# Two neighbouring units in one buffer, loaded by one 2 MB transfer with 4 KB rows

## The reference

```python
Ws = 0.5 * (W + jnp.swapaxes(W, -1, -2))
A = jax.nn.sigmoid(U @ U.T)
K = Ws * A[None, :, :]
deg = jnp.maximum(K.sum(axis=-1), EPS)
d = jax.lax.rsqrt(deg)
K = K * d[:, :, None] * d[:, None, :]
out = layernorm(x + w_scale * jnp.einsum('bnm,bmc->bnc', K, x))
```

## Time and profile before

| | us |
|---|---|
| median of 3 runs | 492.47 |
| lowest, highest | 489.37, 500.56 |
| the profiled execution | 489.78 |
| its span from first to last instruction | 487.9 |

### The profile page before, as it was taken

The page is one execution under the profiler, slowest core; times in us unless marked ns, Lnnn a source line. Parts: engine busy times, 40 slices in busy tenths (PEclk is TensorE's granted clock), DMA queues, the critical chain, the costliest instruction groups (busy, mean ns, idle before and its releaser), DMA issues.

```text
span 487.9 us, 14490 instructions
## 1 busy us (share of the span) xinstructions
PE 447.6 (92%) x5318; PEld 236.5 (48%) x5318; DVE 417.0 (85%) x1154; ACT 209.9 (43%) x655; POOL 113.4 (23%) x133
## 2 busy tenths in 40 slices
PE   7888899999989999999999999799998999899893
PEld 6556344555435553565354554454445544455352
DVE  6897467899699988999899998799889998799745
ACT  3886232554335442554335532454434542444420
POOL 0000011003330225103330234103330225103452
PEclk9996699999999999999999999999999999989998
DMA  8999299986999799996999699976999689984012
GB/s 290 387 330 350 81 362 368 359 301 221 358 343 324 259 321 362 375 326 236 362 380 358 212 380 364 351 241 244 387 345 343 261 322 361 356 253 170 2 41 47
DMA packets 101387, 143.11 MB, mean 293 GB/s; under 512 B 35824, under 2 KB 35824, under 8 KB 101360
## 3 DMA queue, kind: packets, MB, share of 16 engines
q1 hardware_dynamic: 86496, 139.01, 80.7%
q10 hardware_dynamic: 14864, 3.74, 3.6%
HBM read 138.54 MB, written 4.19 MB: 293 GB/s over the span
## 4 chain that ended last, share of the span: by engine, by line
PE 61%; DMA 14%; DVE 12%; issue 8%; ACT 2%; SPq 1%; POOL 0%; DVEq 0%; POOLq 0%
PE yp L437 35%; DMA k<-in_adj_dram 14%; PE tw L395 10%; PE kt L395 9%; DVE k L666 6%; DVE k L677 3%; PE yp L535 3%; PE yp L470 2%; ACT k L559 1%; ACT gate L546 1%; SPq L251 1%; DVE deg_parts L677 1%; DMA h<-in_L_gnn_U_dram 1%; PE kt L481 1%; PE kt L535 0%
## 5 line engine op out<-in xcount | busy, mean ns | idle before, releaser
L559 ACT ACTIVATE k<-kt 128x512 f32<-128x512 f32 (+3 forms) x288 | 149.5, 524 | 234.1 <-PE kt L395 233.8
L437 PE MATMUL yp<-k,z 128*64 128x512 f32 x944 | 239.6, 615 | 4.9 <-DVE z L697 2.6
L666 DVE TENSOR_TENSOR k<-tw,k 128x512 f32<-128x512 f32 (+2 forms) x320 | 193.4, 604 | 41.9 <-PE tw L395 28.5
L677 DVE CUSTOM_DVE_ANT_0 k<-k,gate 128x512 f32<-128x512 f32 (+2 forms) x320 | 198.5, 620 | 0.0
L395 PEld LDWEIGHTS kt<-ident,k 64*128 64x128 f32 x1920 | 75.4, 142 | 86.3 <-issue 86.1
L395 PEld LDWEIGHTS tw<-ident,k 64*128 64x128 f32 x2176 | 83.5, 141 | 67.0 <-issue 65.7
L395 PE MATMUL kt<-ident,k 64*128 64x64 f32 x1920 | 94.2, 232 | 19.5 <-DVE deg_parts L677 13.5
L395 PE MATMUL tw<-ident,k 64*128 64x64 f32 x2176 | 101.7, 230 | 4.5 <-DMA k<-in_adj_dram 1.7
L437 PEld LDWEIGHTS yp<-k,z 128*64 128x64 f32 x944 | 56.4, 137 | 73.1 <-issue 60.0
L327 POOL TENSOR_TENSOR d<-deg,minus_half 128x4 f32<-128x4 f32 x32 | 32.5, 1015 | 222.1 <-DVE deg L687 221.4
L559 ACT ACTIVATION_READ_ACCUMULATOR k<-kt 128x1 f32 x288 | 57.2, 198 | 0.0
(11 more groups left out here) (53 smaller groups left out, 138.7 us busy)
## 6 DMA issues: line engine op xcount, KB each, us to landing
k<-in_adj_dram SPq DMA_DIRECT2D x128, 1024.0 KB, 7.4
xt<-in_x_dram ACTq DMA_DIRECT2D x7, 512.0 KB, 7.6
out_dram<-h SPq DMA_DIRECT2D x7, 512.0 KB, 7.0
xt<-in_x_dram SPq DMA_DIRECT2D x1, 512.0 KB, 14.5
out_dram<-k SPq DMA_DIRECT2D x2, 128.0 KB, 2.1
out_dram<-k SPq DMA_DIRECT2D x3, 64.0 KB, 1.7
h<-in_L_gnn_U_dram SPq DMA_DIRECT2D x1, 128.0 KB, 3.2
out_dram<-k ACTq DMA_DIRECT2D x1, 64.0 KB, 1.9
```

What stands on the lines that cost most here:

```text
L437: t = pe.matmul(yp[at:at + C, m // 2, :], z[:, n * G + c, :], K[(n, m)][:, c, :], start=(q == first_unit[m] and c == 0), stop=(q == last_u ...
L559: nc.scalar.activation(K[(j, i)][:, r, c0:UW].rearrange("p (c h e) -> p c h e", h=2, e=H), whole_rows(kt[:, 0:2, :], r % 2, (UW - c0) // P ...
L666: nc.vector.tensor_tensor(row, whole_rows(tw[:, tw_bank[g] // 2 * 2:tw_bank[g] // 2 * 2 + 2, :], g % 2, w // P), row, ALU.add).then_inc(su ...
L677: nc.vector.tensor_tensor_reduce(row, row, A[:, A_AT[g]:A_AT[g] + w], 1.0, 0.0, ALU.mult, ALU.add, deg_parts[:, i * G + r, j:j + 1]).then_ ...
```

## The change

From batch 1 on, the two units of a pair are loaded by one transfer of 2 MB into one buffer, `wide`, of 128 partitions by 4 rows by 1024, in which both are views; a run in HBM is then 1024 floats (4 KB) in place of 512 (2 KB). One semaphore tells of the pair. A consumer of either unit waits for the whole pair. Batch 0 is still loaded by units, but its last four loads come in another order and with other waits, since the shared memory is laid out anew.

```diff
+FIRST_LOADS = [n for n in FIRST_LOADS if n not in ((2, 2), (2, 3), (3, 2), (3, 3))] + [(3, 2), (3, 3), (2, 3), (2, 2)]
...
-LOADS = [(0, 1), (0, 0)] + [u for pair in PAIRS[1:] for u in pair]
...
-        place = [(2, 2), (3, 3), (3, 2), (2, 3)]
-        place += [n for n in FIRST_LOADS if n not in place]
-        K = {n: sb(f"k_{n[0]}{n[1]}", [P, G, UW]) for n in place}
+        wide_place = [(2, 2), (3, 2)]
+        wide_place += [pair[0] for pair in PAIRS if pair[0] not in wide_place]
+        wide = {n: sb(f"k_{n[0]}{n[1]}", [P, G, 2 * UW]) for n in wide_place}
+        K = {(i, j + k): wide[(i, j)][:, :, k * UW:(k + 1) * UW] for i, j in wide_place for k in range(2)}
...
-        loaded = {n: sem(f"loaded_{n[0]}{n[1]}") for n in LOADS}
+        loaded = {n: sem(f"loaded_{n[0]}{n[1]}") for n in FIRST_LOADS}
+        wide_loaded = {n: sem(f"wide_loaded_{n[0]}{n[1]}") for n in wide_place}
+
+        def wait_loaded(engine, b, n, first):
+            if first:
+                engine.wait_ge(loaded[n], 16)
+            else:
+                engine.wait_ge(wide_loaded[PAIRS[PAIR_OF[n]][0]], b * 16)
...
-                if n in ((3, 2), (2, 3)):
+                if n in ((3, 2), (3, 3)):
                     sp.wait_ge(ut_done, 8)
-                if n in ((2, 2), (3, 3)):
+                if n in ((2, 2), (2, 3)):
                     sp.wait_ge(uu_done, NL)
                 load_unit(0, n)
             def load_pair(b, q):
                 sp.wait_ge(prod_done, b * NQ + (q + 1 - NQ))
-                for n in (LOADS[0:2] if q == 0 else PAIRS[q]):
-                    load_unit(b, n)
+                i, j = PAIRS[q][0]
+                src = adj[b, i * UW:(i + 1) * UW, j * UW:(j + 2) * UW].rearrange("(g p) m -> p g m", p=P)
+                sp.dma_start(wide[(i, j)][:, :, :], src).then_inc(wide_loaded[(i, j)], 16)
...
                 if r == 0:
-                    pe.wait_ge(loaded[(j, i)], b * 16 + 16)
+                    wait_loaded(pe, b, (j, i), first)
...
                 if r == 0:
-                    dve.wait_ge(loaded[STEPS[s]], b * 16 + 16)
+                    wait_loaded(dve, b, STEPS[s], first)
```

More of the change, by code:

```diff
@@ L657, in copy_u, with add_row @@
                 nc.vector.tensor_copy(ut_columns(ut_a, k), ut_bank(2 * k)).then_inc(ut_a_copied, 1)
-            def add_row(b, g):
+            def add_row(b, g, first):
                 s, r = LOWER[g]
@@ L748, in steps @@
                 for g in range(NL):
-                    add_row(b, g)
+                    add_row(b, g, lags == 1)
                     if lags == 1:
```

## The result

The changed kernel takes 544.3 us (median of 4 runs, 541.72 to 548.75), the kernel before 492.6: the ratio is 1.117, with a 95% interval from 1.109 to 1.126. It is slower, in the way that was forecast, but by more: the profiled execution took 542.0 us, where the sum said 531.0, and 1.117 times the time before is 550 us, past the range's 546. Some executions of the changed kernel and of its relatives are longer throughout; the ratios leave them out, and where a median holds some of them the ratio is the better number.

What follows compares the result with a forecast made beforehand. TensorE, VectorE and the DMA engines were taken as nearly full, with nothing to soak up new waits. 489.78 + 31.2 (waits) + 6.8 (clock) + 3.2 (batch 0) = 531.0 us, range 505 to 546.

Steps and rivals of the forecast that it cites:

- The late first unit: Waits for a pair's first unit at rows 4, 12, 16, 28: rows 12, 16, 28 start 2.0, 3.1, 5.3 us later.
- the transfers as the bound: Rival, whole loop: longer rows let the DMA queue run ahead, VectorE's 13.4 us of waits go; 474 us, chance 0.05.
- The idle time: Rival, whole loop: VectorE's 3.3 idle us a period swallow the delays; 493 us, chance 0.06.
- only row 28 counts: Rival, rows 12 to 28: TensorE running ahead makes up rows 12 and 16; 7 x 2.2 us remain, 508 us, chance 0.10.
- Rows of 4 KB do move as packets of 4 KB: Rival, pair loads: claimed the reverse, rows still moved in 2 KB packets, no speed gained; 536 us, chance 0.05.
- half of the 14 as falls: TensorE's two gaps a batch: seven clock falls, five more than now, at 1.35 us each; 6.8 us.
- The rival with all 14: Rival, TensorE's gaps: the clock falls at every gap, 20.4 us; 545 us, chance 0.12.
- The waits were 31.2: Batches 1 to 7: two undisturbed batches 5.1 us longer each, five others 4.2 us each; 31.2 us together.
- 7.55 was said: Pair loads: a pair of 2 MB lands 7.55 us after its issue; ends 5.1 and 7.8.
- lands at 254.9: Row 12, batch 4: q4's load, issued at 246.5, queues behind q3's and lands 5.13 us after it, at 254.9.
- The allowance of 0.9 us: Five batches with a full queue: first units already late, so each grows by 4.2 us where undisturbed ones grow by 5.1.
- Batch 0 was taken at +3.2: Batch 0, TensorE's row 28: unit (2,3) lands at 49.4, 3.2 us late, once; ends 0 and 5.

## Why the forecast was right in kind and too low

**The mechanism held.** The late first unit is the cost: its waits stand where the steps put them (rows 4, 12, 16, 28), and the two runs by units, with and without the pair's wait, show it without any change of transfer. Against the rivals: the transfers as the bound are out, for waits rose fourfold. The idle time did not take the delays in: the period of batch 5 is 7.8 us longer, and with row 28 alone cured 27 of the 58 us of the loss are gone, so not only row 28 counts. Rows of 4 KB do move as packets of 4 KB: the packets from 2 to 8 KB have become 71,792 - 34,928 = 36,864, which is 28,672 for 56 pairs of 512 and 8192 for batch 0.

**The step that failed is the clock.** "I take half of the 14 as falls, five more than now, at 1.35 us each: 6.8 us." The price was about right (1.4 to 1.5 us), the count was wrong. From batch 1 on, without the last 10 us of each trace, the clock falls by 14 pieces of 3.4 us, not 7, against 2 before. After every gap of row 30 in batches 1 to 7 (2.3 to 3.5 us) it is at 0.50, for 3.4 us and in two batches for 6.8. After the gaps at rows 14 and 18 (the transposes of steps 2 and 3) of 1.2 to 1.5 us it is not, nor after one of 1.9; four falls stand at other gaps of 1.8 to 2.9 us, and one in batch 7's end at a gap of 1.1. Twelve pieces more at 1.4 us are 16.8, 10.0 over the term. The rival with all 14, at 545 us, was nearer in time, though not every gap has its fall: row 30 had them all, and the 2.44 us of the earlier trace rows was the row nearest to its gaps.

The length of a gap does not settle it. In the run with q2 and q4 by units, TensorE's row 30 of batches 3 and 6 comes after gaps of 3.10 and 3.21 us, and the clock stays at 1.00; here is batch 3, the transposes and the stretch behind row 28:

```profile
253.55 0.71 PE L412 MATMUL kt<-ident,k 64*128 64x64 f32 x16 [3.10 <-DVE deg_parts L694]
```

```profile
252.01:267.64 15.63, 14.09 (x168) 6.88 (x170) 14.64 (x42) 6.02 (x20) 5.17 (x7) 1.00 0.62 229
```

The changed kernel's second trace has two such gaps as well (3.09 and 3.23 us, in batches 5 and 6). What decides is open.

**The waits were 31.2 and measured some 36.** Batches 1 to 7 grew by 53.2 us (the whole span by 52.3, less batch 0's -0.9, below); without the clock's 16.8 that leaves 36.4. Two landings are behind it. A pair alone lands 7.6 to 7.9 us after its issue, where 7.55 was said. Packets of 4 KB took more than their 171 ns: q1's 71.8% of 16 x 540.2 us are 6206 us, less 20,064 short ones at 18.0 ns (from q10's 3.1%) and 8192 of 2 KB at 90 ns, leaves 5108 us for 28,672, or 178 ns, against 180 for two of 2 KB. On the mean the long rows won almost nothing. And q4, "lands at 254.9", 8.4 us after its issue, took 9.4: 6.0 us behind q3 and not 5.13. That one microsecond passes on. From row 0 on, which is these two lines, batch 4 before and batch 5 after,

```profile
236.18 0.29 DVE L666 TENSOR_TENSOR k<-tw,k 128x128 f32<-128x128 f32 x1 [0.64 <-PE tw L395]
```

```profile
324.49 0.29 DVE L676 TENSOR_TENSOR k<-tw,k 128x128 f32<-128x128 f32 x1 [0.64 <-PE tw L405]
```

rows 12, 16 and 28 come 3.1, 3.7 and 6.4 us later than before, where the steps said 2.0, 3.1 and 5.3. The 6.4 us and the fall's 1.5 are all of the 7.9 us by which batch 5 is longer from row 0 to row 0 (61.45 us against 53.55).

The allowance of 0.9 us for batches with a full queue was wrong in the other direction too: some batches became worse. In batch 4 q2's pair took 9.3 us instead of 7.7, VectorE waited 3.5 us at row 4, and the loop period was 64.3 us. What holds up the queue in such batches is open.

**Batch 0 was taken at +3.2 and measured -0.9.** The wait came, and TensorE's row 28 starts 3.3 us later than its 46.30 before, as said; and yet row 0 of batch 1 starts earlier than the 71.17 us of the kernel before. Two lines of the timeline, TensorE's row 28 of batch 0 and VectorE's row 0 of batch 1:

```profile
49.59 1.12 PE L405 MATMUL tw<-ident,k 64*128 64x64 f32 x16 [4.40 <-DMA k<-in_adj_dram]
...
70.29 0.29 DVE L676 TENSOR_TENSOR k<-tw,k 128x128 f32<-128x128 f32 x1 [2.14 <-PE tw L405]
```

And the stretch of batch 0 in which the clock is low, from the windows:

```profile
47.70:54.50 6.80, 4.91 (x38) 2.71 (x39) 2.51 (x7) 1.27 (x4) 0.00 (x0) 0.50 0.39 143
```

In this execution the clock is low for 6.8 us of batch 0, where it was low for 17.1 us before. Where it is low equally long, the new order costs some 1 us: with 17.1 us row 0 of batch 1 comes at 72.66 us (the run with q2, q4, q5 and q7 by units) against 71.17, and with 13.7 us at 70.36 (the run that waits for both units) against 69.67 (the kernel before with halves). So most of the 3.2 us was taken back, an end that the prediction named, and the shorter stretch of low clock gave the rest, which is luck. Other runs with the same batch 0 reach that row between 69.5 and 76.7 us, with the clock low for 6.8 to 34.1 us.

Together: 489.8 + 36.4 + 16.8 - 0.9 = 542.1, the 542.0 measured. The waits are what was left over, so this sum closes of itself; batch 5, row by row, is the check on it. Of the 11 us that the forecast was short, the clock is 10, the waits are 5, and batch 0 gave 4 back.

## What to carry to other kernels

Before joining two transfers, look at which of the two the consumer waits for: joining takes away no byte, but the first half's data is handed over only with the second's, and where loads are issued just in time that delay comes back in every round. When a chain of waits is cut at one place, look for where the same lateness turns up next: here two short gaps of TensorE became one long one, and nothing was won. Count the falls of the clock as a term of their own, place by place, from the gaps in the trace, and give the count a wide range: gaps of 3.1 us were followed by a fall in one batch and by none in another.

## What was not expected of the hardware

Two transfers of 1 MB with 4 KB rows, split by row blocks, landed 6.9 and 8.9 us after their own issues on an idle queue, where two with 2 KB rows land after 5.0 and 7.3 and one of 2 MB after 7.6 to 7.9. Packets of 4 KB cost 178 ns in the mean, so that doubling the row length gained 1% and not the 5% that the slope from short packets promised.

TensorE's clock stood at 0.50 behind every gap of row 30 in the profiled execution (2.3 to 3.5 us), but at 1.00 behind two gaps of 3.1 and 3.2 us at the same row in the run with q2 and q4 by units.
